# Filling the PSUM banks with h before the projection, in the last stage of a graph-attention kernel

## Chip, cores and metric

One core of a Trainium2 chip. The metric is device microseconds of one execution. The median is over repeated runs; the trace comes from one profiled execution.

## What is computed

x is 8192 by 128 and adj 8192 by 8192, nearly all zeros with a few entries of up to 1e9 in each column. Cut to what matters:

```python
h = maximum(layernorm(x), 0)
proj = einsum('nf,hfo->hno', h, W)            # 4 heads of 128x128
attn = softmax(adj + leaky_relu(s_src + s_tgt), axis=1)
vals = einsum('hij,hjo->hio', attn, proj) + h
out = x + elu(vals).mean(axis=0)
```

The softmax is over the rows of each column and is so peaked that a column gives its whole weight to one row. The kernel finds that row for each column, adds h of the column into the row of a table `sums` in HBM, and projects the sums at the end.

## The kernel before

The matrix is read once, in 23 strips of up to three 128-column sets. VectorE takes maxima, TensorE transposes, ScalarE exponentiates and checks, GpSimd scatters rows of h into `sums` by indirect DMA (L387). A second path for inputs that are not peaked stands behind a flag and isn't run. All of this is the same in both kernels and ends at 830.77 us with the issue of the loads of `sums` (L354, SyncE).

Then comes the last stage. The 64 row tiles are worked off in 32 pairs, w = 0 to 31. A PSUM tile `v_ps[w % 3]` of 128x1024 float32 (two banks) holds one pair: two row tiles by four heads by 128. Each engine has its own list of instructions, executed in order, and waits for the others by semaphores:

- TensorE: `turn_sums(k)` (L471) transposes four tiles of the sums into `agg_ps`; `project(w)` (L481) makes the projection of a pair, recorded as four matmuls of 512 columns. It waits for `stage` and, from w = 3, for the elu of pair w-3 (`t_m`), which frees the bank pair.
- ScalarE: `stage_sums(k)` (L544) copies four transposed tiles to SBUF; L563 takes a quarter of exp(4v - 1) into `e[w % 2]`. Before the loop it multiplies W by 1/4 (L553) and replaces h by h/4 + 1/4 in place (L556, eight instructions).
- VectorE: `add_h(w)` (L704) adds the prepared h to the bank pair, broadcast over the heads; `elu(w)` (L711) is min(e, 1/4) and max with v, from SBUF and PSUM into `m[w % 4]`; `finish(w)` (L717) adds the two SBUF operands, the sum of heads and x, into the output tile. Its loop order is add_h(w), elu(w-1), finish(w-4).
- GpSimd: for each pair two additions in SBUF, four heads to two (`s2`, L400, 512 elements) and two to one (`s1`, L404, 256 elements), each after the one before it.
- SyncE stores four finished tiles at a time (L358).

Ahead of the loop VectorE makes a chain of small checks, each counted in `g_d` (20 in all, last L759). TensorE takes part with L493, and with L495 behind count 18.

Of the kernel before, what the change touches and what calls it, by code (L numbers as in the profile page):

```python
# [6 lines left out]
P = 128  # L7
# [3 lines left out]
ALU = mybir.AluOpType  # L11
ACT = mybir.ActivationFunctionType
# [15 lines left out]
PART = 0.25  # L28
# [57 lines left out]
def peaked_path(nc, ctx, c, W, a_src, a_tgt):  # L86


    N, F, H, O, NT = (c[k] for k in ("N", "F", "H", "O", "NT"))
# [5 lines left out]
    G = 8  # L95
    RT = NT // G
# [17 lines left out]
    PAIRS = NT // 2  # L114

    def sem(name):
        return ctx.enter_context(nc.semaphore(name))
# [109 lines left out]
    t_stage = sem("tail_sums_staged")  # L227
    t_x = sem("tail_x_landed")
    t_part = sem("tail_quarters_ready")
    t_h = sem("tail_h_quarters_ready")  # L230
    t_p = sem("tail_projected")
    t_v = sem("tail_v")
    t_e = sem("tail_exp")
    t_m = sem("tail_elu")
    t_s2 = sem("tail_two_heads")
# [63 lines left out]
    def at(g, i, n):  # L299
        return sets_to(g, i) * G + n  # L300

    def turned_before(g, i, r):

        old = r - AHEAD if r >= AHEAD else r - AHEAD + G
        prior = former_of(g, i) if r >= AHEAD else former_of(*former_of(g, i))
        last = max(n for n, (rr, _) in enumerate(order(subs(*prior))) if rr == old)
        return at(*prior, last + 1)

    def added_before(engine, g, i):

# [9 lines left out]
    with nc.Block() as block:  # L320
# [85 lines left out]
        @block.tensor  # L406
        def _(pe):
            def turn_maxima(g, i, q):
                nq, s = subs(g, i), sets_to(g, i) + q
                pe.wait_ge(f_max, s + 1)  # L410
                if not (first_strip(g, i) and q == 0):
                    pe.wait_ge(f_up, s)
                for u in range(RT):
                    mm = pe.transpose(cells_ps[:, u * P:(u + 1) * P], acc_of(nq)[:, u, q * P:(q + 1) * P], ident[:, :])  # L414
                mm.then_inc(f_mt, 1)

            def turn_idx(g, i):

                pe.wait_ge(f_idx, number(g, i) + 1)
                for q in range(subs(g, i)):  # L420
                    mm = pe.transpose(idx_ps[:, q, :], idx[:, i, q:q + 1].to_broadcast([P, P]), ident[:, :])  # L421
                mm.then_inc(f_idt, 1)

            def sum_same(g, i):

                Q = number(g, i)
                pe.wait_ge(f_same, Q + 1)
                if first_strip(g, i):
                    pe.wait_ge(f_h, NT)
                else:  # L430
                    pe.wait_ge(f_rows, Q)
                for q in range(subs(g, i)):
                    mm = pe.matmul(sum_ps[:, q, :], same[:, q, :],  # L433
                                   h[:, bass.ds(sets_to(g, i) + q, 1), :].rearrange("p t f -> p (t f)"),
                                   start=True, stop=True)
                mm.then_inc(f_sum, 1)

            def turn_chunk(g, i, n):

                nq = subs(g, i)  # L440
                r, q = order(nq)[n]
                pe.wait_ge(f_exp, at(g, i, n) + 1)
                if q == 0:
                    pe.wait_ge(f_in[slot(i, r)], landed(g, i, r))
                for m in range(RT):
                    mm = pe.transpose(turned_ps[n % 2][:, m, :], piece(i, r, nq)[:, m, q * P:(q + 1) * P], ident[:, :])  # L446
                mm.then_inc(f_turn, 1)

            def strip(g, i):
                nq = subs(g, i)  # L450
                turn_maxima(g, i, 0)
                for n in range(EARLY, nq * G):
                    if n % LEAD == LEAD - 1 and n // LEAD + 1 < nq:
                        turn_maxima(g, i, n // LEAD + 1)
                    turn_chunk(g, i, n)
                    if not first_strip(g, i):
                        if n == IDX_AT[nq]:
                            turn_idx(*former_of(g, i))
                        if n == SUM_AT[nq]:
                            sum_same(*former_of(g, i))  # L460
                if not last_strip(g, i):
                    for n in range(EARLY):
                        turn_chunk(*latter_of(g, i), n)

            def turn_sums(k):
                if k * QUAD % RT == 0:
                    pe.wait_ge(t_agg[k * QUAD // RT], 16)
                if k >= 2:
                    pe.wait_ge(t_stage, k - 1)
                for u in range(QUAD):  # L470
                    mm = pe.transpose(agg_ps[k % 2][:, u * P:(u + 1) * P], agg[:, k * QUAD + u, :], ident[:, :])  # L471
                mm.then_inc(t_turn, 1)

            def project(w):
                k = w * 2 // QUAD
                pe.wait_ge(t_stage, k + 1)
                if w >= 3:
                    pe.wait_ge(t_m, w - 2)
                for i in range(2):
                    at = (w * 2 + i) % QUAD * P  # L480
                    mm = pe.matmul(v_ps[w % 3][:, i], stage[:, k % 2, at:at + P], w_part, start=True, stop=True)  # L481
                mm.then_inc(t_p, 1)

            pe.wait_ge(s_ident, 1)
            for n in range(EARLY):
                turn_chunk(0, 0, n)
            strips_of(pe, strip)
            turn_idx((STRIPS - 1) // BODY, (STRIPS - 1) % BODY)
            sum_same((STRIPS - 1) // BODY, (STRIPS - 1) % BODY)

            pe.wait_ge(f_exp, NT * G + 2)
            pe.wait_ge(g_d, 1)
            pe.matmul(check_ps[:, 0:2 * H], ones[:, :], wsq[:, :], start=True, stop=True).then_inc(g_n, 1)  # L493
            pe.wait_ge(g_d, CHECKS - 2)
            pe.transpose(check_ps[0:1, 0:P], bad[:, 0:1], ident[:, :]).then_inc(g_b, 1)  # L495
            pe.wait_ge(f_rows, STRIPS)
            turn_sums(0)
            turn_sums(1)
            pe.wait_ge(g_d, CHECKS)
            pe.wait_ge(t_part, 1)  # L500
            for k in range(NT // QUAD):
                for w in range(k * QUAD // 2, (k + 1) * QUAD // 2):
                    project(w)
                if k + 2 < NT // QUAD:
                    turn_sums(k + 2)

        @block.scalar
        def _(act):
# [31 lines left out]
            def stage_sums(k):  # L540
                act.wait_ge(t_turn, k + 1)
                if k >= 2:
                    act.wait_ge(t_p, (k - 1) * QUAD // 2)
                act.copy(stage[:, k % 2, :], agg_ps[k % 2]).then_inc(t_stage, 1)  # L544

            act.sem_inc(f_exp, 2)
            act.wait_ge(s_const, 1)
            act.activation(h[:, :, F], first.to_broadcast([P, NT]), ACT.Exp, scale=-1.0).then_inc(s_weight, 1)
# [2 lines left out]
            act.wait_ge(f_turn, NT * G)  # L551
            act.wait_ge(s_const, 2)
            act.activation(w_part, w_sb[:, :, :], ACT.Copy, scale=PART).then_inc(t_part, 1)  # L553
            for k in range(G):
                tiles = h[:, k * RT:(k + 1) * RT, 0:F]
                act.activation(tiles, tiles, ACT.Relu, scale=PART, bias=part).then_inc(t_h, 1)  # L556
            stage_sums(0)
            stage_sums(1)
            for w in range(PAIRS):
                act.wait_ge(t_v, w + 1)  # L560
                if w >= 2:
                    act.wait_ge(t_m, w - 1)
                act.activation(e[w % 2], v_ps[w % 3], ACT.Exp, scale=1.0 / PART, bias=e_bias).then_inc(t_e, 1)  # L563
                k = w * 2 // QUAD + 2
                if w % 2 == 1 and k < NT // QUAD:
                    stage_sums(k)

        @block.vector
        def _(dve):
# [128 lines left out]
                if not last_strip(g, i):  # L698
                    piece_max(*after, 6)

            def add_h(w):
                dve.wait_ge(t_p, w + 1)
                dve.wait_ge(t_h, w * 2 // RT + 1)
                dve.tensor_tensor(v_ps[w % 3], h[:, 2 * w:2 * w + 2, 0:F].unsqueeze(2).to_broadcast([P, 2, H, O]),  # L704
                                  v_ps[w % 3], ALU.add).then_inc(t_v, 1)

            def elu(w):
                dve.wait_ge(t_e, w + 1)
                if w >= 4:
                    dve.wait_ge(t_s2, w - 3)  # L710
                dve.scalar_tensor_tensor(m[:, w % 4], e[w % 2], PART, v_ps[w % 3],  # L711
                                         ALU.min, ALU.max).then_inc(t_m, 1)
# [45 lines left out]
            done(dve.tensor_reduce(flag_f[0:1, 0:1], check_ps[0:1, 0:P], AX.X, ALU.max))  # L758
            done(dve.tensor_copy(flag[:, :], flag_f[0:1, 0:1]))  # L759
            assert count[0] == CHECKS  # L760
            dve.wait_ge(t_x, 16 * (RING - LAST_SLOT))
            for w in range(PAIRS + 4):
                if w < PAIRS:
                    add_h(w)
                if 1 <= w < PAIRS + 1:
                    elu(w - 1)
                if w >= 4:
                    finish(w - 4)


def dense_path(nc, ctx, c):
# [306 lines left out]
```

## Time and profile before

| | us |
|---|---|
| median of 3 runs | 935.72 |
| lowest and highest | 931.46, 936.46 |
| the profiled execution | 935.8 |
| its span, first to last instruction | 934.1 |
| VectorE busy | 805.6 |
| TensorE busy | 710.0 |
| ScalarE busy | 682.9 |
| GpSimd busy | 288.6 |
| mean granted TensorE clock, share of full | 0.929 |

The span is the time between the first and the last instruction; the execution's own time is 1.7 us more. Busy times are sums over the whole span, and engines overlap. The last stage takes the stretch from 830.77 us to the end.

### The profile page before, as it was taken

The numbers are of one execution on the slowest core, as the hardware profiler recorded it, in microseconds if no ns is written. First come the engines' busy times: TensorE is split into PE (matmuls) and PEld (weight loads), VectorE is DVE, ScalarE is ACT, GpSimd is POOL, SyncE is SP. The second block draws the span as 40 slices with busy tenths as digits, with TensorE's granted clock in tenths as the row PEclk, the third lists the DMA queues.
The fourth block names the chain that finished last, engine by engine and source line by source line (L and its number), as shares of the span: only waits on it lengthen the run. The fifth ranks groups of instructions, "written<-read, shape, count | busy, mean of one in ns | idle before, by whom it ended". The sixth has DMA issues, their size and how long they took to land.

```text
span 934.1 us, 14971 instructions
## 1 busy us (share of the span) xinstructions
PE 710.0 (76%) x4995; PEld 576.0 (62%) x4995; DVE 805.6 (86%) x812; ACT 682.9 (73%) x1173; POOL 288.6 (31%) x164
## 2 busy tenths in 40 slices
PE   1507687987887987988987987888898888838882
PEld 1506576776776776777776766776686776613330
DVE  3886888999988999988999999999988995429996
ACT  0498577977977977977977887887886887755552
POOL 1000202332332232432232432432332422227885
PEclk8657989999999999999999999999999999969997
DMA  9999999999999999999999999999999996853112
GB/s 250 332 375 392 373 346 372 348 366 375 370 360 374 350 368 374 372 360 372 354 367 372 373 370 369 374 370 371 372 369 354 363 278 147 222 116 98 56 46 58
DMA packets 224100, 294.93 MB, mean 316 GB/s; under 512 B 4544, under 2 KB 218048, under 8 KB 224064
## 3 DMA queue, kind: packets, MB, share of 16 engines
q1 hardware_dynamic: 214848, 290.27, 90.7%
q0 software_dynamic: 9216, 4.20, 3.7%
q8 instruction: 20, 0.33, 0.2%
q14 instruction: 16, 0.13, 0.0%
HBM read 281.80 MB, written 12.65 MB: 315 GB/s over the span
## 4 chain that ended last, share of the span: by engine, by line
PE 36%; issue 16%; ACT 13%; DVE 12%; DMA 11%; POOL 6%; SPq 4%; ACTq 0%; POOLq 0%; DVEq 0%
PE ps L446 27%; ACT ps L517 12%; PE ps L414 7%; DMA sums<-arena 6%; DMA arena<-in_adj 5%; DVE arena L597 5%; POOL arena L400 4%; DVE ps L602 3%; SPq L343 3%; DVE arena L580 3%; POOL arena L404 2%; SPq L328 1%; PE ps L433 1%; DVE arena L601 1%; PE ps L421 1%
## 5 line engine op out<-in xcount | busy, mean ns | idle before, releaser
L517 ACT ACTIVATE ps<-ps,arena 128x1024 f32<-128x1024 f32 x512 | 556.1, 1086 | 180.7 <-DVE arena L601 110.6
L446 PE MATMUL ps<-ident,arena 128*128 128x128 f32 x4096 | 560.4, 285 | 75.9 <-ACT ps L517 57.9
L446 PEld LDWEIGHTS ps<-ident,arena 128*128 128x128 f32 x4096 | 463.8, 145 | 161.9 <-ACT ps L517 137.9
L580 DVE TENSOR_TENSOR arena<-arena 128x3072 f32<-128x3072 f32 (+2 forms) x115 | 359.3, 3125 | 13.3 <-DMA arena<-in_adj 10.2
L387 POOL DMA_INDIRECT sums<-arena x64 | 175.6, 2744 | 530.3 <-DVE arena L636 230.7
L414 PE MATMUL ps<-ident,arena 128*128 128x128 f32 x512 | 75.2, 295 | 104.0 <-DVE ps L602 61.8
L414 PEld LDWEIGHTS ps<-ident,arena 128*128 128x128 f32 x512 | 62.6, 152 | 111.0 <-issue 67.2
L597 DVE TENSOR_REDUCE arena<-ps 128x1 f32<-128x1024 f32 x64 | 78.4, 1225 | 45.5 <-PE ps L414 43.7
L517 ACT ACTIVATION_READ_ACCUMULATOR ps<-ps,arena 128x1 f32 x512 | 100.5, 196 | 0.0
L576 DVE TENSOR_TENSOR arena<-arena 128x3072 f32<-128x3072 f32 (+2 forms) x23 | 71.8, 3124 | 14.7 <-DMA arena<-in_adj 14.7
L602 DVE SCALAR_TENSOR_TENSOR ps<-ps,arena 128x1024 f32<-128x1024 f32 x64 | 82.1, 1282 | 0.3 <-issue 0.3
L589 DVE TENSOR_TENSOR arena<-arena 128x1024 f32<-128x1024 f32 x64 | 76.4, 1222 | 3.7 <-DMA arena<-in_adj 2.7
L380 POOL COPY arena<-arena 128x27 f32 (+3 forms) x23 | 55.0, 2391 | 77.3 <-DMA sums<-arena 77.3
L481 PE MATMUL ps<-arena 128*128 128x512 f32 x128 | 63.4, 619 | 11.9 <-DVE arena L711 11.9
L563 ACT ACTIVATE arena<-ps,arena 128x1024 f32<-128x1024 f32 x32 | 35.7, 1115 | 41.1 <-DVE ps L704 41.1
L400 POOL TENSOR_TENSOR arena<-arena 128x512 f32<-128x512 f32 x32 | 44.0, 1375 | 26.3 <-DVE arena L711 26.3
L481 PEld LDWEIGHTS ps<-arena 128*128 128x128 f32 x128 | 22.3, 193 | 43.9 <-issue 43.7
L704 DVE TENSOR_TENSOR ps<-arena,ps 128x1024 f32<-128x1024 f32 x32 | 38.8, 1214 | 10.1 <-PE ps L481 10.1
L711 DVE SCALAR_TENSOR_TENSOR arena<-arena,ps 128x1024 f32<-128x1024 f32 x32 | 38.5, 1204 | 0.0
L530 ACT ACTIVATE arena<-arena,nmr,rstd x64 | 27.3, 494 | 3.5 <-DVE nmr L671 3.5
L404 POOL TENSOR_TENSOR arena<-arena 128x256 f32<-128x256 f32 x32 | 23.9, 746 | 2.5
L433 PE MATMUL ps<-arena 128*128 (+1 forms) x128 | 18.2, 276 | 0.4 <-DVE arena L626 0.4
(74 smaller groups left out, 184.0 us busy)
## 6 DMA issues: line engine op xcount, KB each, us to landing
arena<-in_adj SPq DMA_DIRECT2D x160, 1536.0 KB, 14.5
arena<-in_adj SPq DMA_DIRECT2D x16, 512.0 KB, 7.2
arena<-in_adj SPq DMA_DIRECT2D x8, 1024.0 KB, 8.5
sums<-arena SPq DMA_DIRECT2D x1, 4160.0 KB, 22.4
arena<-sums SPq DMA_DIRECT2D x8, 512.0 KB, 7.2
out<-arena SPq DMA_DIRECT2D x16, 256.0 KB, 2.3
sums<-arena POOLq DMA_INDIRECT x64, 8.4
w_sb<-in_L_gnn_W SPq DMA_DIRECT2D x1, 256.0 KB, 2.9
```

What stands on the lines that cost most here:

```text
L380: pool.tensor_copy(hist[:, bass.ds(sets_to(g, i), nq), :], cert[:, i, 0:nq, :]).then_inc(f_kept, 1)
L387: pool.indirect_dma_start(sums, bass.IndirectOffsetOnAxis(target[:, i, q:q + 1], 0), rows[:, i, q, 0:F], None, compute_op=ALU.add).then_in ...
L400: pool.tensor_tensor(s2[w % 4], m[:, w % 4, :, 0:2, :], m[:, w % 4, :, 2:4, :], ALU.add).then_inc(t_s2, 1)
L414: mm = pe.transpose(cells_ps[:, u * P:(u + 1) * P], acc_of(nq)[:, u, q * P:(q + 1) * P], ident[:, :])
L446: mm = pe.transpose(turned_ps[n % 2][:, m, :], piece(i, r, nq)[:, m, q * P:(q + 1) * P], ident[:, :])
L481: mm = pe.matmul(v_ps[w % 3][:, i], stage[:, k % 2, at:at + P], w_part, start=True, stop=True)
L517: act.activation(turned_ps[n % 2], turned_ps[n % 2], ACT.Exp, scale=KAPPA, bias=cert[:, i, q, G:G + 1], accum_out=cert[:, i, q, r:r + 1]). ...
L576: dve.tensor_tensor(acc_of(nq), piece(i, 0, nq), piece(i, 1, nq), ALU.max).then_inc(f_acc, 1)
L580: dve.tensor_tensor(acc_of(nq), acc_of(nq), piece(i, r, nq), ALU.max).then_inc(f_acc, 1)
L589: dve.tensor_tensor(acc_of(nq)[:, :, cols], acc_of(nq)[:, :, cols], piece(i, G - 1, nq)[:, :, cols], ALU.max).then_inc(f_max, 1)
L597: dve.tensor_reduce(cmx[:, i, q:q + 1], cells_ps[:, :], AX.X, ALU.max).then_inc(f_mx, 1)
L602: dve.scalar_tensor_tensor(cells_ps[:, :], cells_ps[:, :], cmx[:, i, q:q + 1], place, ALU.is_equal, ALU.mult, accum_out=in_range[:, i, q:q ...
```

## The change

VectorE's `add_h` and its semaphore go, as does ScalarE's preparation of h in place. Instead the bank pair is filled with h/4 + 1/4 before the projection, which adds onto it (`start=False`). Bank pairs 0 and 1 are filled by ScalarE, bank pair 2 by VectorE. Six extra matmul calls (`open_banks`) write each bank once beforehand with `start=True`, so that later matmuls find them in the accumulating state. ScalarE's exponential now waits for the projection, and VectorE's order becomes elu(w), a fill after every third pair, finish(w-3).

```diff
             def project(w):
                 pe.wait_ge(t_stage, k + 1)
-                if w >= 3:
-                    pe.wait_ge(t_m, w - 2)
+                if w % 3 == 2:
+                    pe.wait_ge(t_fd, w // 3 + 1)
+                else:
+                    pe.wait_ge(t_fa, w // 3 * 2 + w % 3 + 1)
...
-                    mm = pe.matmul(v_ps[w % 3][:, i], stage[...], w_part, start=True, stop=True)
+                    mm = pe.matmul(v_ps[w % 3][:, i], stage[...], w_part, start=False, stop=True,
+                                   skip_group_check=True)
+            def open_banks(b):
+                for i in range(2):
+                    mm = pe.matmul(v_ps[b][:, i], ident[:, :], w_sb[:, :, :], start=True, stop=True)
+                mm.then_inc(t_open, 1)
...
             pe.matmul(check_ps[:, 0:2 * H], ones[:, :], wsq[:, :], start=True, stop=True).then_inc(g_n, 1)
+            pe.wait_ge(f_up, NT)
+            open_banks(0)
+            open_banks(2)
             pe.wait_ge(g_d, CHECKS - 2)
             pe.transpose(check_ps[0:1, 0:P], bad[:, 0:1], ident[:, :]).then_inc(g_b, 1)
+            pe.wait_ge(g_d, CHECKS)
+            open_banks(1)
             pe.wait_ge(f_rows, STRIPS)
...
+            def fill(w):
+                act.wait_ge(t_open, 1 if w % 3 == 0 else 3)
+                if w >= 3:
+                    act.wait_ge(t_m, w - 2)
+                act.activation(v_ps[w % 3], h_of(w), ACT.Relu, scale=PART, bias=part).then_inc(t_fa, 1)
...
-            for k in range(G):
-                tiles = h[:, k * RT:(k + 1) * RT, 0:F]
-                act.activation(tiles, tiles, ACT.Relu, scale=PART, bias=part).then_inc(t_h, 1)
+            fill(0)
+            fill(1)
             stage_sums(0)
             stage_sums(1)
             for w in range(PAIRS):
-                act.wait_ge(t_v, w + 1)
+                act.wait_ge(t_p, w + 1)
                 ...
+                if (w + 2) % 3 != 2 and 3 <= w + 2 < PAIRS:
+                    fill(w + 2)
...
-            def add_h(w):
-                dve.wait_ge(t_p, w + 1)
-                dve.wait_ge(t_h, w * 2 // RT + 1)
-                dve.tensor_tensor(v_ps[w % 3], h[:, 2 * w:2 * w + 2, 0:F].unsqueeze(2).to_broadcast([P, 2, H, O]),
-                                  v_ps[w % 3], ALU.add).then_inc(t_v, 1)
+            def fill(w):
+                dve.wait_ge(t_open, 2)
+                if w >= 3:
+                    dve.wait_ge(t_m, w - 2)
+                dve.tensor_scalar(v_ps[w % 3], h_of(w), PART, PART, ALU.mult, ALU.add).then_inc(t_fd, 1)
...
+            fill(2)
             dve.wait_ge(t_x, 16 * (RING - LAST_SLOT))
-            for w in range(PAIRS + 4):
+            for w in range(PAIRS + 3):
                 if w < PAIRS:
-                    add_h(w)
-                if 1 <= w < PAIRS + 1:
-                    elu(w - 1)
-                if w >= 4:
-                    finish(w - 4)
+                    elu(w)
+                if w % 3 == 2 and w + 3 < PAIRS:
+                    fill(w + 3)
+                if w >= 3:
+                    finish(w - 3)
```

## Rows read from the trace of the kernel before

**Rows 1.** Page: busy us, share of the span and instructions of each engine.
```profile
PE 710.0 (76%) x4995; PEld 576.0 (62%) x4995; DVE 805.6 (86%) x812; ACT 682.9 (73%) x1173; POOL 288.6 (31%) x164
```

**Rows 2.** Windows, last stage: busy us of engines, granted clock, DMA share, GB/s.
```profile
860.00:880.00 20.00, 16.61 (x47) 7.04 (x46) 20.00 (x25) 10.82 (x12) 16.18 (x17) 1.00 0.18 52
```

**Rows 3.** Groups by line, 851 to 925 us: busy us, mean ns, idle before.
```profile
L711 DVE SCALAR_TENSOR_TENSOR arena<-arena,ps 128x1024 f32<-128x1024 f32 x28 | 33.7, 1203 | 0.0
L563 ACT ACTIVATE arena<-ps,arena 128x1024 f32<-128x1024 f32 x27 | 30.1, 1115 | 34.3 <-DVE ps L704 34.3
L544 ACT COPY arena<-ps 128x512 f32<-128x512 f32 x12 | 6.9, 577 | 0.0
```

**Rows 4.** Timeline of one pair in the loop: start us, duration us.
```profile
858.53 0.41 DVE L717 SCALAR_TENSOR_TENSOR arena<-arena 128x256 f32<-128x256 f32 x1
858.69 1.40 POOL L400 TENSOR_TENSOR arena<-arena 128x512 f32<-128x512 f32 x1 [0.41 <-DVE arena L711]
858.87 1.22 DVE L704 TENSOR_TENSOR ps<-arena,ps 128x1024 f32<-128x1024 f32 x1
860.00 1.21 DVE L711 SCALAR_TENSOR_TENSOR arena<-arena,ps 128x1024 f32<-128x1024 f32 x1
860.17 0.73 POOL L404 TENSOR_TENSOR arena<-arena 128x256 f32<-128x256 f32 x1
860.55 0.60 PE L471 MATMUL ps<-ident,arena 128*128 128x128 f32 x4
861.13 0.41 DVE L717 SCALAR_TENSOR_TENSOR arena<-arena 128x256 f32<-128x256 f32 x1
861.29 1.39 POOL L400 TENSOR_TENSOR arena<-arena 128x512 f32<-128x512 f32 x1 [0.39 <-DVE arena L711]
861.35 1.96 PE L481 MATMUL ps<-arena 128*128 128x512 f32 x4 [0.21 <-DVE arena L711]
```

**Rows 5.** Timeline ahead of and into the loop, 820 to 845 us.
```profile
820.75 0.29 PE L493 MATMUL ps<-arena,ones 128*128 128x8 f32 x2
821.65 8.41 ACT L556 ACTIVATE arena<-arena 128x1024 f32<-128x1024 f32 x8
829.43 0.37 PE L495 MATMUL ps<-ident,arena 128*1 128x128 f32 x1 [8.39 <-DVE arena L756]
830.23 0.14 DVE L759 CAST flag<-arena 1x1 int32<-1x1 f32 x1
834.97 1.94 PE L471 MATMUL ps<-ident,arena 128*128 128x128 f32 x8 [5.16 <-DMA arena<-sums]
836.82 4.83 PE L481 MATMUL ps<-arena 128*128 128x512 f32 x8
840.13 1.23 DVE L704 TENSOR_TENSOR ps<-arena,ps 128x1024 f32<-128x1024 f32 x1 [9.77 <-PE ps L481]
841.40 1.11 ACT L563 ACTIVATE arena<-ps,arena 128x1024 f32<-128x1024 f32 x1 [3.87 <-DVE ps L704]
842.82 1.22 DVE L711 SCALAR_TENSOR_TENSOR arena<-arena,ps 128x1024 f32<-128x1024 f32 x1
844.12 1.27 POOL L400 TENSOR_TENSOR arena<-arena 128x512 f32<-128x512 f32 x1 [15.00 <-DVE arena L711]
```

**Rows 6.** The instructions of L556: duration ns min/median/max, first and last start.
```profile
L556 ACT ACTIVATE arena<-arena x8: 1133/1135/1137, 821.6 to 828.9; 128x1024 f32<-128x1024 f32 x8
```

**Rows 7.** Timeline of the end of the loop, 922 to 926 us.
```profile
922.50 1.18 POOL L404 TENSOR_TENSOR arena<-arena 128x256 f32<-128x256 f32 x1
923.63 1.26 POOL L400 TENSOR_TENSOR arena<-arena 128x512 f32<-128x512 f32 x1
923.70 1.47 DVE L717 SCALAR_TENSOR_TENSOR arena<-arena 128x256 f32<-128x256 f32 x1 [0.62 <-POOL arena L404]
925.79 0.43 DVE L717 SCALAR_TENSOR_TENSOR arena<-arena 128x256 f32<-128x256 f32 x1 [0.61 <-POOL arena L404]
```

**Rows 8.** Windows around TensorE's clock: columns as in Rows 2.
```profile
822.50:823.00 0.50, 0.00 (x0) 0.00 (x0) 0.00 (x0) 0.50 (x2) 0.00 (x0) 0.50 0.00 0
838.50:839.00 0.50, 0.50 (x2) 0.34 (x1) 0.00 (x0) 0.00 (x0) 0.00 (x0) 0.50 1.21 291
839.25:839.50 0.25, 0.25 (x2) 0.16 (x1) 0.00 (x0) 0.00 (x0) 0.00 (x0) 1.00 1.24 293
```

More of the change, by code:

```diff
@@ L229, in peaked_path @@
     t_part = sem("tail_quarters_ready")
-    t_h = sem("tail_h_quarters_ready")
-    t_p = sem("tail_projected")
-    t_v = sem("tail_v")
+    t_open = sem("tail_banks_open")
+    t_fa = sem("tail_h_filled_by_scalar")
+    t_fd = sem("tail_h_filled_by_vector")
+    t_p = sem("tail_v")
     t_e = sem("tail_exp")
@@ L307, in turned_before, with h_of @@
         return at(*prior, last + 1)
+    def h_of(w):
+        return h[:, 2 * w:2 * w + 2, 0:F].unsqueeze(2).to_broadcast([P, 2, H, O])
     def added_before(engine, g, i):
@@ L476, in project @@
                 pe.wait_ge(t_stage, k + 1)
-                if w >= 3:
-                    pe.wait_ge(t_m, w - 2)
+                if w % 3 == 2:
+                    pe.wait_ge(t_fd, w // 3 + 1)
+                else:
+                    pe.wait_ge(t_fa, w // 3 * 2 + w % 3 + 1)
                 for i in range(2):
                     at = (w * 2 + i) % QUAD * P
-                    mm = pe.matmul(v_ps[w % 3][:, i], stage[:, k % 2, at:at + P], w_part, start=True, stop=True)
+                    mm = pe.matmul(v_ps[w % 3][:, i], stage[:, k % 2, at:at + P], w_part, start=False, stop=True,
+                                   skip_group_check=True)
                 mm.then_inc(t_p, 1)
+            def open_banks(b):
+                for i in range(2):
+                    mm = pe.matmul(v_ps[b][:, i], ident[:, :], w_sb[:, :, :], start=True, stop=True)
+                mm.then_inc(t_open, 1)
             pe.wait_ge(s_ident, 1)
@@ L498, in _ @@
             turn_sums(1)
-            pe.wait_ge(g_d, CHECKS)
             pe.wait_ge(t_part, 1)
```

## Prediction, made before the changed kernel was run

> **What bounds the kernel now.** I read the busy shares first [rows 1]. They average over a long matrix pass that this change does not touch, so they say nothing about it. The stretch windows of the last stage do [rows 2]: of 20.00 us VectorE is busy 20.00, TensorE 16.61, GpSimd 16.18, ScalarE 10.82. The groups of that stage say the same from the other side [rows 3]: VectorE's elu has no idle time ahead of it, ScalarE's exp has 34.3 us, all of it waiting for `add_h`. The loop is VectorE's. The timeline gives the period [rows 4]: finish at 858.53 and again at 861.13, 2.60 us per pair. It splits by start-to-start distances into finish 0.34 (to 858.87), add_h 1.13 (to 860.00) and elu 1.13 (to 861.13). The durations (0.41, 1.22, 1.21) overlap by some 0.08 each, so distances are the prices in a queue that is full, and durations the prices in a chain.
>
> **What is removed.** One VectorE instruction of 1.13 per pair, 32 times: 36 us of the bounding engine, so the bound moves. L556's 8.41 us on ScalarE goes too, at no gain: it starts at 821.65, and ScalarE's next work needs the transposes that start at 834.97, which wait for the loads of the sums [rows 5].
>
> **What is added ahead of the loop.** Four `open_banks` calls (banks 0 and 2) come behind L493 at 820.75. A projection of four matmul records takes 1.96 at full clock [rows 4], so a bank pair takes 2.0, or 4.0 at half clock, and two take 4.0 to 8.0: done by 825 to 829.1, before L495 at 829.43. Bank pair 1 is opened after the last check (830.23 + 0.14), done by 832.4 to 834.4; the first transposes start at 834.97. Both are covered, the second by 0.6 at the least; without the cover it would cost at most 3.4. The fills: ScalarE's two take 1.135 each [rows 6], the one of bank 1 ending by about 835.6; `stage_sums(0)`, behind it in the queue, needs the first four of the eight transposes (1.94 from 834.97), so it could not start before about 835.9. VectorE's is at 830.4, where it is idle. The chain of scatter DMAs and loads that ends at 834.97 has no new work in its way: no queue of SyncE or GpSimd gets an instruction more. So nothing moves before 834.97.
>
> **The first pair.** The projection of pair 0 is visible to VectorE at 840.13. Then come add_h 1.23, exp 1.11 (from 841.40), elu (from 842.82, which had queued behind the second add_h) and GpSimd at 844.12 [rows 5]. Now exp starts at 840.13, elu at 840.13 + 1.11 + 0.03 = 841.27, and GpSimd at 841.27 + 1.22 + 0.08 = 842.57. That is **1.55 us** earlier.
>
> **The period afterwards.** Five resources bid for it.
>
> *VectorE*: elu 1.13, finish 0.34, a third of a fill. A fill is not in the trace as a tensor_scalar of this size. Its upper bound is add_h's 1.22 (one operand more), its lower bound half of that, 0.6. I take 1.13 as the distance, since it is nearest to add_h in size and target. Sum 1.13 + 0.34 + 0.38 = 1.85.
>
> *TensorE*: two projections of 1.96 and one set of transposes of 0.60 for two pairs [rows 4]: at most 2.26.
>
> *ScalarE*: a full queue of 1024-element activations has distances of (8.41 - 1.135) / 7 = 1.04 [rows 5, 6], copies 0.577 - 0.08 = 0.50 [rows 3]. Six pairs hold 6 exp, 4 fills and 3 copies: 11.9, or 1.98 a pair. But fills and exps aren't independent. In each round of three pairs the fill of the second bank is issued before one exp, and its own projection and exp follow. From the fill's start to that exp: 1.13 + 0.14 + 1.96 = 3.23; ScalarE has only 2.08 to do meanwhile, or 2.58 where a copy falls there. The stalls are 1.15 and 0.65 in six pairs. (11.9 + 1.8) / 6 = **2.28**.
>
> *GpSimd*: s2 took 1.27 when no finish ran beside it [rows 5], then 0.08 to s1, 0.73. That is 2.08. So far ScalarE's loop would set the end.
>
> *GpSimd with VectorE's finish.* Look at s2 once more: 1.39 and 1.40 in the loop where a finish had started 0.16 before it [rows 4], and 1.27 without. At the end [rows 7] a finish that started 0.07 after an s2 took 1.47 instead of 0.41 and ended at 925.17, 0.28 after that s2's end at 924.89. An s1 that met two finishes took 1.18 instead of 0.73. They don't share, each waits for the whole of the other. Before, GpSimd had 0.40 of idle time, and finish fell into it. Now GpSimd is close to full, and the finish needs a hold of its own of 0.28 to 0.34 (the 0.28 just worked out; its distance 0.34). GpSimd's loop is 2.08 + 0.3 = **2.38**, the largest bid. The Trainium skill, "SBUF — State Buffer", on engine ports, says a VectorE operation with two SBUF inputs and a GpSimd operation that reads SBUF exclude each other for a whole instruction. The trace agrees with its 1.47. By the same page an operation with one SBUF input, outside the two-port modes, stays free of it, as the elu is; no row here tests the fill.
>
> I take 2.38. The bounds are 2.28 (finishes fall into gaps) and 1.39 + 0.08 + 0.73 + 0.28 = 2.48 (a finish delays both additions).
>
> **The sum.** Before, s2 went from 844.12 to 923.63 in 31 steps: 79.5 us. After: 31 x 2.38 = 73.8, so 5.7 less. The first three steps have no finish beside them and run at 2.28, another 0.3. The drain is the same: from the last s2's start two additions and a finish, 923.63 to 926.22, and the last store and the end of the execution behind it. 1.55 + 5.7 + 0.3 = 7.55. From the profiled execution's 935.8 this gives 928.25. The median is 0.08 lower, so **928.2 us**.
>
> **A term left at zero: the clock.** TensorE is at half clock from 822.50 on, and returns to full only at about 839.1, some 4.1 us after it became busy at 834.97 [rows 5, 8]. Projection 0, which begins at 836.82, therefore runs mostly at half clock. `open_banks(1)` makes TensorE busy from 830.4 to about 834, with a gap of about 1 us before 834.97. The clock may come back sooner. Bounds: nothing, or projection 0 wholly at full clock, 840.13 - 836.82 = 3.31 against 1.96, so 1.35. I take nothing, as TensorE was likewise idle about 1 us before the clock fell (L493's end at 821.04 to half clock at 822.50, with the exact moment between).
>
> **Rivals.**
> 1. *The finish holds VectorE up* (slower). If it is issued just behind the start of an s2 each time, as at 923.70, VectorE's pair is 1.13 + 1.26 + 0.34 + 0.38 = 3.11, and 31 x 0.51 = 15.8 longer, less 1.55: 950. For it: the lock is in the trace, and GpSimd is busy most of the time. Against it: s2(w) can't start before elu(w) ends, and the finish is issued 0.08 before that, so it meets an s2 only when GpSimd is a pair behind; then the wait of VectorE lets GpSimd catch up. It decides once the finish waits on average more than 2.60 - 1.13 - 0.34 - 0.38 = 0.75 us.
> 2. *Both additions and the finish hinder one another always* (no change). s2 at 1.39 and s1 at 1.18, as seen once [rows 7], give 1.39 + 0.08 + 1.18 = 2.65. The loop stays where it was and only the first pair's 1.55 is left: 934.2.
> 3. *ScalarE's loop is the bound and the clock returns early*: 31 x 0.10 = 3.1 and 1.35 less: 923.8.
> 4. *The accumulating matmul is slower than the overwriting one.* No row shows such a matmul. Bounds: no difference, or as at half clock, 1.96 to 3.92 a pair, over 4.2 with transposes: 31 x 1.6 = 50 more, 985. Nothing in the trace speaks for it.
>
> **How the numbers follow.** Chances: the forecast 0.60, rival 3 or a part of it 0.18, rival 2 0.15, rival 1 0.05, rival 4 0.02. The range goes from 923.3 (rival 3's 923.8, and 0.5 below it for the spread of the runs) to 932.0 (period 2.48, 31 x 0.10 = 3.1 more, and 0.7 for that spread, which before was 931.46 to 936.46). About 0.5% is what tells a change from none here, 4.7 us, the border at 931.0. Faster takes the forecast, most of its upper edge, and rival 3: 0.77. Same takes rival 2 and a bit of the forecast: 0.17. Slower takes rivals 1 and 4, less a mild case: 0.06.
>
> **What would show it.** The first exp at about 840.1. A distance of 2.3 to 2.45 between s2's. GpSimd busy over 0.9 of the loop's windows, VectorE no longer at 20 of 20 unless its finishes are stretched: their mean should be well above 0.41, and no longer all alike, in a pattern of three pairs. A stall of about 1 us before one exp in three on ScalarE. Wrong would be: finishes that all last above 1.2 (rival 1), s2's spaced 2.6 (rival 2), matmul distances above 0.45 in the loop (rival 4), any movement of the 834.97 mark, or a ScalarE fill much over 1.135.

## The result, and the profile after

The changed kernel takes 926.16 us (median of 6 runs, 925.54 to 927.15), the kernel before 936.17 beside it. The ratio is 0.9896, 95% interval 0.9878 to 0.9914: faster, by some 9.7 us by that ratio. The forecast was 928.2 in a range of 923.3 to 932.0.

The profiled execution took 926.4 us, 9.4 less than before. First the page's busy times:

```profile
PE 713.4 (77%) x5007; PEld 577.6 (62%) x5007; DVE 788.5 (85%) x790; ACT 696.0 (75%) x1187; POOL 286.9 (31%) x164
```

Against [rows 1] VectorE lost 17.1 us and ScalarE gained 13.1. The groups of the loop, 846 to 915 us (busy us, mean ns, idle before and its releaser), answer to [rows 3]:

```profile
L404 POOL TENSOR_TENSOR arena<-arena 128x512 f32<-128x512 f32 x30 | 39.5, 1317 | 5.4 <-DVE arena L737 5.3
L737 DVE SCALAR_TENSOR_TENSOR arena<-arena,ps 128x1024 f32<-128x1024 f32 x30 | 36.4, 1213 | 8.0 <-ACT arena L586 8.0
L586 ACT ACTIVATE arena<-ps,arena 128x1024 f32<-128x1024 f32 x29 | 32.2, 1111 | 8.7 <-PE ps L487 8.2
L408 POOL TENSOR_TENSOR arena<-arena 128x256 f32<-128x256 f32 x30 | 23.6, 786 | 2.4
L568 ACT ACTIVATE ps<-arena 128x1024 f32<-128x1024 f32 x19 | 21.5, 1130 | 1.0 <-DVE arena L737 0.9
L743 DVE SCALAR_TENSOR_TENSOR arena<-arena 128x256 f32<-128x256 f32 x31 | 19.3, 628 | 0.0
L731 DVE TENSOR_SCALAR ps<-arena 128x1024 f32<-128x1024 f32 x9 | 11.0, 1227 | 1.0
```

L737 is elu, L586 exp, L568 and L731 the fills, L404 and L408 are GpSimd's two additions (s2 and s1), L743 is finish. ScalarE's idle time ahead of exp fell from 34.3 us to 8.7. VectorE now waits 8.0 us for ScalarE. And the finish, alike in almost every pair before at 0.41 us, is 0.63 on average. The windows of 860 to 880 us, the counterpart of [rows 2]:

```profile
860.00:880.00 20.00, 17.90 (x54) 8.14 (x52) 18.04 (x21) 17.32 (x20) 17.51 (x18) 1.00 0.19 55
```

TensorE 17.90, VectorE 18.04, ScalarE 17.32, GpSimd 17.51 of 20 us. No engine is full: the four lie between 87% and 90% of the window, and each waits for another somewhere. Now the way into the loop, as a timeline (start us, duration us):

```profile
829.94 1.23 DVE L731 TENSOR_SCALAR ps<-arena 128x1024 f32<-128x1024 f32 x1
829.96 3.78 PE L494 MATMUL ps<-w_sb,ident 128*128 128x512 f32 x4 [0.61 <-DVE flag L785]
830.44 11.18 SPq L358 DMA_DIRECT2D arena<-sums  x8
833.78 1.12 ACT L568 ACTIVATE ps<-arena 128x1024 f32<-128x1024 f32 x1 [10.11 <-PE ps L494]
834.68 1.94 PE L475 MATMUL ps<-ident,arena 128*128 128x128 f32 x8 [0.94 <-DMA arena<-sums]
839.63 1.11 ACT L586 ACTIVATE arena<-ps,arena 128x1024 f32<-128x1024 f32 x1 [2.40 <-PE ps L487]
840.86 1.22 DVE L737 SCALAR_TENSOR_TENSOR arena<-arena,ps 128x1024 f32<-128x1024 f32 x1 [9.69 <-ACT arena L586]
842.16 1.27 POOL L404 TENSOR_TENSOR arena<-arena 128x512 f32<-128x512 f32 x1 [13.49 <-DVE arena L737]
```

TensorE's openings and VectorE's fill end before the transposes start at 834.68; ScalarE's second fill ends at 834.90, before the first copy at 835.80 (its first, for bank pair 0, was over long before). Against [rows 5] everything is 0.3 earlier (830.44 against 830.77 for the loads). That is chance in the part ahead, which the change does not touch: the changed kernel's second trace, the last run below, has the loads at 829.51. The loads' issue is therefore the mark that I measure the stage from: to the end of the last finish it took 95.45 us before (830.77 to 926.22) and takes 86.44 (830.44 to 916.88), **9.0 less**.

The first s2 comes 1.63 earlier from that mark. Its 31 steps take 71.96 us (842.16 to 914.12), against 79.51. That is 2.32 per pair. Inside the loop, from the tenth to the twenty-eighth s2, the distance (from the start of one s2 to that of the next) is 2.355, against 2.597 before. Here is a stretch of the loop, with lines of TensorE and some of ScalarE left out:

```profile
866.64 1.23 DVE L731 TENSOR_SCALAR ps<-arena 128x1024 f32<-128x1024 f32 x1
866.72 0.72 POOL L408 TENSOR_TENSOR arena<-arena 128x256 f32<-128x256 f32 x1
867.40 1.26 POOL L404 TENSOR_TENSOR arena<-arena 128x512 f32<-128x512 f32 x1
867.77 1.18 DVE L743 SCALAR_TENSOR_TENSOR arena<-arena 128x256 f32<-128x256 f32 x1
868.88 1.21 DVE L737 SCALAR_TENSOR_TENSOR arena<-arena,ps 128x1024 f32<-128x1024 f32 x1
868.92 1.11 ACT L586 ACTIVATE arena<-ps,arena 128x1024 f32<-128x1024 f32 x1 [1.10 <-PE ps L487]
870.01 0.41 DVE L743 SCALAR_TENSOR_TENSOR arena<-arena 128x256 f32<-128x256 f32 x1
870.16 1.39 POOL L404 TENSOR_TENSOR arena<-arena 128x512 f32<-128x512 f32 x1 [0.62 <-DVE arena L737]
```

Read it from the top. VectorE's fill pushes the finish behind it to 867.77, into an s2 that runs from 867.40 to 868.66. The finish lasts 1.18 instead of 0.41 and ends 0.29 after that s2. The elu queued behind it starts only at 868.88, and GpSimd, which needs that elu, idles 0.62 until 870.16. The distance between these two s2's is 2.76; the two after it are 2.27 and 2.03, with no idle time on GpSimd, and so it goes on in rounds of three pairs: 7.06, or 2.355 a pair. VectorE's fill itself disturbs nobody: the s1 beside it takes 0.72.

On ScalarE one exp in six pairs waits 1.10 for its projection, as forecast (1.15), and one 0.57 (0.65):

```profile
875.82 1.11 ACT L586 ACTIVATE arena<-ps,arena 128x1024 f32<-128x1024 f32 x1 [0.57 <-PE ps L487]
877.25 1.12 ACT L568 ACTIVATE ps<-arena 128x1024 f32<-128x1024 f32 x1 [0.31 <-DVE arena L737]
```

The second line is the place where the two engines' loops touch: a fill that waits for an elu that came late.

### The profile page after: what moved, and what is told of

Its sections match the earlier page's. It is cut to its first block, busy times and chain, and to the rows that moved or that the text cites. A ratio compares the mean times of both kernels' runs of the same rounds, so it can differ in the third digit from the quotient of the medians.

```text
span 924.6 us, 14987 instructions
## 1 busy us (share of the span) xinstructions
PE 713.4 (77%) x5007; PEld 577.6 (62%) x5007; DVE 788.5 (85%) x790; ACT 696.0 (75%) x1187; POOL 286.9 (31%) x164
## 4 chain that ended last, share of the span: by engine, by line
PE 40%; issue 16%; ACT 14%; DVE 11%; DMA 8%; POOL 5%; SPq 4%; ACTq 0%; POOLq 0%; DVEq 0%
PE ps L450 31%; ACT ps L534 13%; PE ps L418 7%; DMA arena<-in_adj 5%; DVE arena L622 5%; POOL arena L404 4%; DMA sums<-arena 3%; DVE ps L627 3%; SPq L347 3%; DVE arena L605 1%; PE ps L437 1%; SPq L332 1%; POOL arena L408 1%; PE ps L425 1%; DVE arena L626 1%
## 5 line engine op out<-in xcount | busy, mean ns | idle before, releaser
L737 DVE SCALAR_TENSOR_TENSOR arena<-arena,ps 128x1024 f32<-128x1024 f32 x32 | 38.8, 1214 | 18.1 <-ACT arena L586 18.1
L404 POOL TENSOR_TENSOR arena<-arena 128x512 f32<-128x512 f32 x32 | 42.1, 1315 | 18.9 <-DVE arena L737 18.8
L586 ACT ACTIVATE arena<-ps,arena 128x1024 f32<-128x1024 f32 x32 | 35.6, 1111 | 11.8 <-PE ps L487 11.2
L568 ACT ACTIVATE ps<-arena 128x1024 f32<-128x1024 f32 x22 | 24.9, 1130 | 12.2 <-PE ps L494 11.3
L408 POOL TENSOR_TENSOR arena<-arena 128x256 f32<-128x256 f32 x32 | 25.1, 784 | 2.5
L743 DVE SCALAR_TENSOR_TENSOR arena<-arena 128x256 f32<-128x256 f32 x32 | 19.7, 622 | 0.6 <-POOL arena L408 0.6
```

What stands on the lines that cost most here:

```text
L404: pool.tensor_tensor(s2[w % 4], m[:, w % 4, :, 0:2, :], m[:, w % 4, :, 2:4, :], ALU.add).then_inc(t_s2, 1)
```

## The experiments

Each timing below is given with the kernel before that was run beside it. Where a kernel was timed once, I go by the trace: the distance of s2's inside the loop (tenth to twenty-eighth) and the length of the stage from the issue of the loads to the end of the last finish. The changed kernel has 2.355 us and 86.44 us. A single time says less, since the loads themselves are issued anywhere from 828.1 to 832.9 us in these runs.

### A finish with one SBUF operand

```diff
-                dve.scalar_tensor_tensor(osb[:, tiles, :], s1[:, w % 4], -1.0, x_rows[...][...],
-                                         ALU.add, ALU.add).then_inc(t_o, 1)
+                dve.tensor_reduce(osb[:, tiles, :], s1[:, w % 4].unsqueeze(3), AX.X, ALU.add).then_inc(t_o, 1)
```

> The changed kernel, with finish as a tensor_reduce over one element: same 256 outputs, but one SBUF operand in place of two. It leaves out the addition of x and -1. Reference is the changed kernel's own trace: s2 to s2 2.32 us per pair (842.16 to 914.12 in 31 steps), finish 628 ns on average. Theory, VectorE and GpSimd exclude each other over the finish: all finishes about 0.41 or less, s2 always 1.27, distance down to ScalarE's loop of 2.28, so 1.3 us less over 31 steps and up to 2.2 us in all. Rival, the finish only lasts long because of something else (its wait for s1): mean finish and distance stay at 0.63 and 2.32.

Distance 2.285, 31 steps 69.92 us (2.0 less), stage 83.71 (2.7 less, of which 0.5 is an earlier first exp by the clock). Timed once, 925.98 us against 934.29; its loads were issued at 832.90, 2.5 later than in the changed kernel. The groups of 846 to 910 us, and one meeting in the timeline:

```profile
L743 DVE TENSOR_REDUCE arena<-arena 128x256 f32<-128x256 f32 x27 | 11.1, 411 | 0.0
L404 POOL TENSOR_TENSOR arena<-arena 128x512 f32<-128x512 f32 x28 | 35.7, 1274 | 6.2 <-DVE arena L737 6.2
```

```profile
868.90 1.27 POOL L404 TENSOR_TENSOR arena<-arena 128x512 f32<-128x512 f32 x1
869.62 0.41 DVE L743 TENSOR_REDUCE arena<-arena 128x256 f32<-128x256 f32 x1
```

A finish that starts in the middle of an s2 now lasts 0.41, and s2 is never more than 1.29 (1.274 on average). The theory held; the rival, that the wait for s1 stretched the finish, fell. The distance went to 2.285, the 2.28 forecast for ScalarE's loop.

The two traces also show where the difference of 0.07 lies. Over six pairs ScalarE takes 14.13 us in the changed kernel (fill at 863.12 to fill at 877.25) and 13.71 here (864.98 to 878.69). The waits for projections are the same, 1.10 and 0.57 in the one, 1.11 and 0.57 in the other. All of the 0.42 stands in one place, ahead of the fill at 877.25: it starts 1.43 after the exp before it, and 1.02 after it here, where the elu is not late.

### Half of the projection, and both edits

```diff
-                for i in range(2):
+                for i in range(1):
                     at = (w * 2 + i) % QUAD * P
                     mm = pe.matmul(v_ps[w % 3][:, i], stage[:, k % 2, at:at + P], w_part, start=False, ...)
```

> The changed kernel, projecting only the first tile of each pair: two matmul records a pair, 0.98 us in place of 1.96. Half of the output lacks its projection. Theory, the exclusion around the finish sets the distance and ScalarE's loop is just beneath it: distance stays at 2.3 to 2.34 although the stalls of ScalarE for the projection vanish; only the first pair is 0.9 earlier. Rival, ScalarE's loop through the projection sets it alone: distance falls to 2.1, 6 to 7 us less.

> Both edits of the two runs before: a finish with one SBUF operand and half of the projection (leaves out x, -1 and half of the projection). Theory, two limits stand side by side, the exclusion (2.32 to 2.34) and ScalarE's loop (2.28): only with both gone does the distance fall far, to GpSimd's own 2.08 or 2.10, some 7 to 8 us less than the changed kernel. Rival, they are one limit or neither is: no lower than the lower of the two single edits.

Half of the projection alone: distance 2.356, unchanged. With both: 2.224, and 31 steps in 66.81 us (2.155 each), 5.1 less than the changed kernel. Timed once, they took 922.60 and 922.02 us against 934.29. The stages were 83.31 and 79.95 us; TensorE's early clock gave the first of these more than the expected 0.9 (its transposes took 1.06 instead of 1.94). In the groups of the first of the two kernels:

```profile
L586 ACT ACTIVATE arena<-ps,arena 128x1024 f32<-128x1024 f32 x27 | 30.0, 1110 | 5.4 <-PE ps L487 5.4
L568 ACT ACTIVATE ps<-arena 128x1024 f32<-128x1024 f32 x18 | 20.3, 1126 | 5.0 <-DVE arena L737 5.0
L743 DVE SCALAR_TENSOR_TENSOR arena<-arena 128x256 f32<-128x256 f32 x29 | 18.4, 636 | 0.0
```

ScalarE's waiting did not go, it changed its address: less for TensorE, 5.0 us for VectorE's elu ahead of the fills. The finish is still 0.636. But TensorE's clock also fell to half for stretches of these runs, and there half of a projection took 2.04 (863.37 to 865.41), as long as a whole one at full clock. So the rounds have to be looked at one by one (windows of three pairs, granted clock third from the end; then the fill):

```profile
852.49:859.56 7.07, 4.79 (x15) 1.90 (x14) 6.48 (x8) 5.70 (x6) 6.21 (x6) 0.98 0.17 49
859.56:866.63 7.07, 4.35 (x9) 2.22 (x10) 6.49 (x8) 5.86 (x7) 6.22 (x7) 0.76 0.22 64
859.58 1.12 ACT L568 ACTIVATE ps<-arena 128x1024 f32<-128x1024 f32 x1 [1.38 <-DVE arena L737]
```

The first round of three pairs ran at a granted clock of 0.98 and no exp in it waited for a projection; the fill that ends it waited 1.38 for the elu instead. The second ran at 0.76 and one exp waited 1.20. Both took 7.07, the changed kernel's 7.06. So the exclusion sets the distance, and ScalarE's loop through the projection stands 0.07 beneath it. The theory expected 2.08 to 2.10 with both gone, and that figure was missed by 0.13. Most of it is the clock. Six pairs at full clock (s2 at 861.75 to 874.47) took 12.72 us, 2.12 each; six at a granted clock of 0.87 (880.75 to 894.41) took 13.66, 2.28 each. What is left over 2.10 is 0.02.

### Every finish twice

```diff
+                dve.scalar_tensor_tensor(agg[:, tiles, :], s1[:, w % 4], -1.0, x_rows[...][...],
+                                         ALU.add, ALU.add)
                 dve.scalar_tensor_tensor(osb[:, tiles, :], s1[:, w % 4], -1.0, x_rows[...][...],
                                          ALU.add, ALU.add).then_inc(t_o, 1)
```

> The changed kernel with every finish made twice, the first time into memory that is no longer needed. VectorE's own work per pair goes from 1.85 to 2.19, still under 2.28. Theory, exclusion: each further finish with two SBUF operands waits for a GpSimd addition or delays one; worked through with the durations of the trace the distance is 3.1 and the kernel 23 us slower, slower than the kernel before. Rival, the finishes share and only their sum counts: 2.3, within 1 us of the changed kernel.

947.60 us against 934.29, each timed once: slower than the kernel before. Distance 3.136, stage 110.26, 23.8 more than the changed kernel, for 32 instructions whose own distance is 0.34, 11 us in sum. The timeline shows where the rest comes from (L743 and L745 are the two finishes):

```profile
887.81 0.41 DVE L743 SCALAR_TENSOR_TENSOR arena<-arena 128x256 f32<-128x256 f32 x1
887.97 1.38 POOL L404 TENSOR_TENSOR arena<-arena 128x512 f32<-128x512 f32 x1 [0.62 <-DVE arena L737]
888.14 1.48 DVE L745 SCALAR_TENSOR_TENSOR arena<-arena 128x256 f32<-128x256 f32 x1
889.42 0.79 POOL L408 TENSOR_TENSOR arena<-arena 128x256 f32<-128x256 f32 x1
889.55 1.21 DVE L737 SCALAR_TENSOR_TENSOR arena<-arena,ps 128x1024 f32<-128x1024 f32 x1
```

The first finish slips in ahead of s2 and delays it to 1.38. The second comes 0.17 behind its start and ends 0.27 after it. This is rival 1 of the prediction, produced on purpose: the fast loop and a loop slower than before are one 0.34 us instruction apart.

### The same finish in the kernel before

The edit of the first experiment, made to the kernel before.

> The kernel before, with finish as a tensor_reduce with one SBUF operand (leaves out x and -1). Theory: before the change the finish fell into GpSimd's idle time, so the exclusion cost nothing: s2 shrinks from 1.39 to 1.27 but the distance stays at 2.60 in the loop (2.565 over all 31), last stage the same within 0.5 us. Rival: the exclusion cost the kernel before as well, and part of the change's gain is that it did not: distance under 2.55.

Distance 2.588 against 2.597: the exclusion cost that kernel next to nothing in its loop, because its finish fell into GpSimd's 0.4 us of idle time (now 0.51, with every s2 at 1.27). The change used up that idle time. The 31 steps took 78.67 us against 79.51, 0.8 less, mostly in the last step (2.03 against 2.61), where an s1 had met finishes and taken 1.18 [rows 7]. The stage, 95.09 against 95.45, hides half of that, since the first s2 came 0.56 later behind the loads. Timed once, 933.88 us against 936.19.

### Who makes the fills

First all on ScalarE, none on VectorE (the first three fills and TensorE's waits are changed to match, here and below; not shown):

```diff
-                if (w + 2) % 3 != 2 and 3 <= w + 2 < PAIRS:
+                if 3 <= w + 2 < PAIRS:
                     fill(w + 2)
...
-                if w % 3 == 2 and w + 3 < PAIRS:
-                    fill(w + 3)
```

> The changed kernel with all fills on ScalarE (none on VectorE). ScalarE's queue per pair: exp 1.04, fill 1.04, half a copy 0.25, together 2.33 without any stall, VectorE's 1.47 plus waits. Theory (ScalarE becomes the bound, the exclusion is absorbed by VectorE's idle time): distance 2.33 to 2.37, time within 1.5 us of the changed kernel. Rival (VectorE's fill was what made the finishes late): distance falls under 2.28.

926.69 us, ratio 0.9922 (0.9900 to 0.9945); distance 2.377, stage 86.88. ScalarE busy 39.27 of 40 us between 860 and 900. One bound was put in the place of another at the same height, as expected. Its finishes last 0.42, and its s2's 1.38.

Then all on VectorE, none on ScalarE:

```diff
-                if (w + 2) % 3 != 2 and 3 <= w + 2 < PAIRS:
-                    fill(w + 2)
...
-                if w % 3 == 2 and w + 3 < PAIRS:
+                if w + 3 < PAIRS:
                     fill(w + 3)
```

> The changed kernel with all fills on VectorE: the addition of h is then a fill of the same length, only earlier. VectorE per pair: 1.13 + 1.13 + 0.34 = 2.60 as before, with waits at the finish on top. Theory (the gain is that two fills of three left VectorE; the accumulation as such gives nothing): distance 2.6 to 2.75, so no faster than the kernel before, at most 1.5 us faster through the first pair and up to 3 us slower. Rival (taking add_h out of the chain between projection and exp is what gained): most of the 9.7 us is kept.

938.80 us, ratio 1.0034 (1.0016 to 1.0051), slower than the kernel before by a third of a per cent. Distance 2.789, a little over the expected 2.75; first exp as early as in the changed kernel. The waits at the finish that were expected on top of 2.60 are not there (0.42 in the loop). The 0.19 lies between elu and fill: `fill(w + 3)` waits for the end of the elu just ahead of it in the same queue, and starts 1.32 after it (870.53 to 871.85) instead of 1.13. The changed kernel pays that once in three pairs (865.31 to 866.64). So moving the addition ahead of the projection gains nothing by itself, the first pair aside. What gained is that two fills of three went to an engine that had 34 us of idle time. A fill lasts as long on VectorE as add_h did (1.227 and 1.214).

### Fills to ScalarE, copies to VectorE

Besides the edit with all fills on ScalarE, VectorE gets the copies from k = 2 on, and ScalarE's are dropped there:

```diff
+            def stage_sums(k):
+                dve.wait_ge(t_turn, k + 1)
+                dve.wait_ge(t_p, (k - 1) * QUAD // 2)
+                dve.tensor_copy(stage[:, k % 2, :], agg_ps[k % 2]).then_inc(t_stage, 1)
...
                 if w < PAIRS:
                     elu(w)
+                k = w * 2 // QUAD + 2
+                if w % 2 == 1 and k < NT // QUAD:
+                    stage_sums(k)
```

> All fills on ScalarE, and in exchange the copies of the transposed sums (from k = 2) on VectorE behind every second elu. ScalarE per pair 2.08, VectorE 1.13 + 0.34 + 0.3 = 1.77 plus waits, GpSimd 2.08 plus 0.3 for the finish where it does not fall into a gap. Theory: ScalarE has no stall left for a projection, since each fill is followed by a whole exp and a whole fill; distance 2.13 (between 2.1 and 2.38), 4 to 6 us faster than the changed kernel, ratio to the kernel before about 0.984. Rival (the exclusion bounds at 2.38 whatever ScalarE does): no gain on the changed kernel.

922.56 us (921.13 to 923.04, 4 runs), ratio 0.9865 (0.9847 to 0.9883). Distance 2.162, stage 81.80, 4.6 less than the changed kernel. The windows of 860 to 900 us (TensorE, its loads, VectorE, ScalarE, GpSimd) and finish's group:

```profile
860.00:900.00 40.00, 38.45 (x112) 16.96 (x111) 39.40 (x47) 39.73 (x39) 38.59 (x38) 1.00 0.22 64
```

```profile
L742 DVE SCALAR_TENSOR_TENSOR arena<-arena 128x256 f32<-128x256 f32 x31 | 22.4, 726 | 0.0
```

All four engines are at 96% or more, and yet the finish is longer than in any kernel above that makes it once, 0.726. GpSimd has no idle time ahead of any s2 between 866 and 905 us and so shows what finishes cost it when it is full: distances of 2.10 and 2.16 in turn (2.13 on average from the fourteenth s2 on), where pairs without a finish beside them take 2.03. A finish that waits for an s2 lengthens the s1 after it from 0.73 to 0.79; one that is running when an s1 starts makes that s1 0.85. My 2.38 was therefore no bound: the finish costs GpSimd about 0.1 a pair and not 0.3; the longer part of the meeting is VectorE's. The rival, no gain on the changed kernel, fell.

### The openings and the clock

```diff
-            open_banks(0)
-            open_banks(2)
+            pe.sem_inc(t_open, 2)
...
-            open_banks(1)
+            pe.sem_inc(t_open, 1)
```

> The changed kernel without the six matmuls that open the banks (the sums may then overwrite the fills, so the output is not to be relied on). Theory: they lie in idle time and cost nothing, and matmul timing does not depend on whether it accumulates: the first exp, the distance 2.32 and the time are the same within 0.5 us. Rival: they shift the loads or the first projection, up to 1.4 us.

Distance 2.356, matmuls at 601 ns against 602, stage 86.91, 0.5 more: first exp 9.66 from the loads instead of 9.19. The openings cost nothing. The full clock came back later here, 5.3 us after the start of the transposes instead of 4.1; whether that is owed to their absence one run can't say. Timed once, 929.42 us: not the same within 0.5 as expected, but 2.0 of the 3.3 more is the loads, issued at 832.46.

```diff
             pe.wait_ge(g_d, CHECKS)
+            pe.matmul(v_ps[1][:, 0], ident[:, :], w_sb[:, :, :], start=True, stop=True)
             open_banks(1)
```

> The changed kernel with one more opening matmul of 512 columns (two records) ahead of the opening of bank pair 1, so that TensorE is busy from about 830 without a break up to the transposes at about 834.7. Theory (the gap before the transposes is why the clock returned only 4.1 us after them): full clock at about 834 to 835, the projection of pair 0 wholly at full clock, first exp about 1.3 earlier after the start of the transposes (from 4.95 to 3.7 us), the transposes at most 0.5 late. Rival: the clock returns when it did, 4.1 us after the transposes, and nothing is gained.

The windows (granted clock is the third number from the end) and ScalarE's timeline:

```profile
834.00:835.00 1.00, 1.00 (x2) 0.18 (x1) 0.00 (x0) 0.00 (x0) 0.00 (x0) 0.50 1.22 298
835.00:836.00 1.00, 1.00 (x8) 0.75 (x7) 0.00 (x0) 0.51 (x1) 0.00 (x0) 0.82 1.21 288
836.00:837.00 1.00, 0.34 (x4) 0.10 (x1) 0.00 (x0) 1.00 (x2) 0.00 (x0) 1.00 1.22 291
```

```profile
835.49 1.13 ACT L569 ACTIVATE ps<-arena 128x1024 f32<-128x1024 f32 x1 [12.14 <-PE ps L494]
836.55 1.06 ACT L562 COPY arena<-ps 128x512 f32<-128x512 f32 x2
839.23 1.11 ACT L587 ACTIVATE arena<-ps,arena 128x1024 f32<-128x1024 f32 x1 [1.61 <-PE ps L487]
```

The clock came back at about 835.4, while it returned at about 838.8 in the changed kernel, and the projection ran at full clock. But the fill of bank 1 had to wait for the longer opening and stood ahead of the first copy, which came at 836.55 instead of 835.80. First exp 8.73 after the loads, 0.45 earlier and not 1.3. Stage 86.00, distance 2.357, 926.03 us timed once. And even the 0.45 is not clearly the opening's: the first experiment's kernel, with the changed kernel's openings, also had its first exp 8.73 after the loads, its clock being back 3.3 us after the start of the transposes.

> Fills on ScalarE, copies on VectorE, and the one more opening. Theory: the two add up, the distance of 2.16 and an earlier first exp: ratio to the kernel before 0.984 to 0.986, 3 to 5 us faster than the changed kernel. Rival: clock not earlier, the same as fills and copies alone (0.9865).

923.36 us, ratio 0.9853 (0.9828 to 0.9877), inside the expected 0.984 to 0.986 and yet not to be told from the rival's 0.9865, the version without the additional opening. Its four times go from 921.32 to 925.28, and the trace is of the longest. In it the clock was back at about 836.3 and lost again:

```profile
837.00:838.00 1.00, 0.65 (x6) 0.41 (x4) 0.00 (x0) 1.00 (x2) 0.00 (x0) 1.00 1.22 289
838.00:839.00 1.00, 0.00 (x0) 0.00 (x0) 0.00 (x0) 1.00 (x2) 0.00 (x0) 1.00 1.22 290
839.00:840.00 1.00, 0.41 (x1) 0.41 (x2) 0.00 (x0) 0.97 (x2) 0.00 (x0) 0.85 1.22 291
840.00:841.00 1.00, 1.00 (x2) 0.34 (x1) 0.00 (x0) 0.00 (x0) 0.00 (x0) 0.50 1.22 290
```

TensorE idled from 837.65 to 839.59, behind ScalarE's fills and copies, and the clock fell just after the projection had started, some 2.0 us after the idleness began. First exp 11.16 us after the loads. In this execution the two did not add up; whether they do in the faster ones no trace shows.

### The changed kernel once more

> The changed kernel again, unaltered, timed beside the candidate for a better version: ratio to the kernel before 0.9896 within 0.002, distance of s2's 2.32. If fills on ScalarE with copies on VectorE is truly better, the two intervals stand apart.

926.41 us, ratio 0.9891 (0.9871 to 0.9911), distance 2.356. The candidate's interval (0.9847 to 0.9883) overlaps with this one by 0.0012 and with the first measurement's by 0.0005. So the intervals do not stand apart, which was the mark set beforehand. The median is 3.6 to 3.9 us lower, but 2.4 to 2.9 by the ratios, as the kernel before was faster beside it too (934.73 against 936.17 and 936.19). The stage in the trace is 4.6 us shorter, and its cause is seen there. Fills on ScalarE with copies on VectorE is therefore most likely better than the changed kernel, by 0.3 to 0.5%; the timings alone do not settle it.

## Why the prediction was right, and where not

**Ahead of the loop, right.** Nothing moved, the transposes started 4.24 us after the loads, against 4.20. The openings of two bank pairs took 3.68 us, under the lower bound of the 4.0 to 8.0 given, and the third 3.78, within 2.0 to 4.0.

**The first pair, right.** 1.55 forecast, 1.63 measured from the loads.

**Prices, right.** ScalarE's fill 1.130 (1.135 forecast), VectorE's 1.227 (1.22 was the upper bound; the distance to the next instruction is 1.13 to 1.14, as taken). Left out was the 0.19 by which VectorE's fill waits for the elu ahead of it: 0.06 a pair.

**The period, 2.38 against 2.355 in the loop.** Nearly the number, by a partly wrong way, and so in part by luck. The cause, that finish and GpSimd's additions exclude each other, is shown: take it away and the distance is 2.285, double it and it is 3.136. The Trainium skill's rule on the shared port ("SBUF — State Buffer", on engine ports) is borne out by this and by the tensor_reduce with one SBUF operand, which shared freely. But the step that failed is the sum "2.08 + 0.3", a GpSimd that is full and carries each finish on top. Both terms were too large: a pair without a finish beside it takes GpSimd 2.03, and a finish adds about 0.1. GpSimd was busy 17.5 of 20 us and idled 0.62 once in three pairs. The cost arises on VectorE: one finish in three waits for an s2, and the elu behind it comes late. The round is 2.27 + 2.03 + 2.76 = 7.06: two steps at GpSimd's pace, and one (s2 of 1.26, the 0.29 to the end of the finish, elu of 1.21) through VectorE. That is the mechanism of rival 1, which I had priced for every pair and so given 0.05; it is there in one pair of three. With fills and copies laid out otherwise, GpSimd ran at 2.16.

**ScalarE's loop, 2.28, right.** It appeared at 2.285 as soon as the exclusion was gone, with stalls of 1.11 and 0.57 where 1.15 and 0.65 were forecast. The prediction did not see that this loop can be relieved by handing ScalarE all the fills and taking the copies from it.

**The 31 steps, 6.0 forecast against 7.55.** The stage lost 9.0 us where 7.55 was forecast, and this is the missing 1.5. The medians differ by 10.0; of the 2.0 between 928.2 and 926.16 the rest is within what the part ahead varies by. The first three steps took 6.63 instead of 6.84, the middle 24 took 56.7 instead of 57.1, and the last four, 8.6 instead of 9.5:

```profile
905.50 1.39 POOL L404 TENSOR_TENSOR arena<-arena 128x512 f32<-128x512 f32 x1 [0.63 <-DVE arena L737]
907.77 1.27 POOL L404 TENSOR_TENSOR arena<-arena 128x512 f32<-128x512 f32 x1
909.88 1.26 POOL L404 TENSOR_TENSOR arena<-arena 128x512 f32<-128x512 f32 x1
912.03 1.26 POOL L404 TENSOR_TENSOR arena<-arena 128x512 f32<-128x512 f32 x1
914.12 1.44 POOL L404 TENSOR_TENSOR arena<-arena 128x512 f32<-128x512 f32 x1
```

No copy is left there and no fill of VectorE's, whose place in the round was what pushed the finish into an s2; ScalarE's last fill starts at 907.58. The distance falls to 2.1 behind the first of them. The last pairs of a loop are cheaper than its middle, and I had given them the middle's price. The rest of the stage, the drain, took 2.76 instead of 2.59.

**The clock term, zero, right by luck.** Measured from the transposes' start the full clock returned after 4.1 us in both kernels (834.97 to 839.1, 834.68 to 838.8). But other kernels with the same openings had it back after 3.3 us (the first experiment) or already before the transposes (half of the projection: about 832.3, with the first exp 6.67 us after the loads). With the other half of the projection at full clock, 0.98 more, that would be 7.65 instead of 9.19: an estimate of 1.5 for what the term can be worth, a little over its upper bound of 1.35, since the transposes were faster too (1.06 against 1.94).

**Rivals.** Rival 2 (no change) needed both additions and the finish to hinder one another always; mean s2 was 1.317 and s1 0.786, not 1.39 and 1.18. Rival 3 came half-way: ScalarE's loop was next, 0.07 below the distance, and the clock did not return early. Rival 4 is out: 0.43 between the weight loads of the accumulating matmuls, and 602 ns per matmul against 611.

## What to carry to other kernels

When the bounding engine is relieved, the distance can go to a loop through several engines, as here, and not to the next engine's sum; find the round in which one instruction is issued just ahead of what it must feed. Idle time of an engine that costs nothing may still be what hides a conflict with another engine: look for one instruction with two durations (0.41 and 1.47 here) before counting that time as free. Once four engines stand within a few per cent, which engine does which small piece decides: the same additions on VectorE made 1.0034, divided 0.9896, and exchanged for the copies 0.9865.

## What was not expected of the hardware

A finish that waits for a GpSimd addition costs VectorE up to 1.1 us and GpSimd only 0.06: it ends 0.28 after the addition, and the next addition is longer by 0.06 (0.79 against 0.73). An addition that starts while a finish runs is longer by 0.12 (1.39 against 1.27, 0.84 against 0.73).

TensorE's full clock outlived idleness after the first openings: full until about 828.6, though TensorE had been idle from 824.2. In the kernel before it was lost at about 822.1, 1 us after the last work. The two kernels with one more opening had it back before the projection, and one of them lost it again; the kernel with half of the projection had it back there too, without one. A gain in clock at the entrance of a stage is real but not steady.
